# Attention over 164 keys on one core: three products of the last 36 keys in one matmul, the mean's rows ahead of the low halves, six batches' text statistics moved into batch 0

## The reference

```python
xn = layernorm(layernorm(h)) * ln_w
Q = xn[:, None] * W_qk[None, :, None]                 # 12 heads, Q = K
attn = softmax(causal(einsum('bhse,bhte->bhst', Q, Q) / sqrt(192)))
out = einsum('bhst,bhte->bhse', attn, xn[:, None] - mean(wte, axis=0))
h = h + (out / arange(1, 165)).reshape(b, s, 12 * 192) @ W_o.T
h = h + switch_moe(layernorm(h))                      # 16 experts, capacity 64, wi 192x768, wo 768x192
```

## Time and profile before

| | |
|---|---|
| median of 3 runs | 353.12 us (350.88 to 353.52) |
| the profiled execution | 352.87 us, its span 351.0 us |
| mean granted TensorE clock | 0.984 |
| PE busy | 328.0 us, 93% of the span, 2352 matmuls |
| DVE busy | 226.3 us, 64% |
| POOL busy | 166.5 us, 47% |
| ACT busy | 125.4 us, 36% |
| DMA moved | 74.35 MB, mean 212 GB/s |

### The profile page before, as it was taken

How to read it: one execution, slowest core, us unless ns; L and a number is a source line. 1 busy time by engine, 2 the same in 40 slices (tenths; PEclk the granted TensorE clock), 3 DMA queues, 4 the chain that set the end, 5 groups by cost and what they waited for, 6 DMA issues and landing times.

```text
span 351.0 us, 6745 instructions
## 1 busy us (share of the span) xinstructions
PE 328.0 (93%) x2352; PEld 304.0 (87%) x2352; DVE 226.3 (64%) x562; ACT 125.4 (36%) x437; POOL 166.5 (47%) x180
## 2 busy tenths in 40 slices
PE   8998998999999999999998996999988999999991
PEld 3696996997998998989987985999867999999991
DVE  2788696797796887787888959457676522222220
ACT  1466427434525545354362041545620111011110
POOL 3476746657559549648555013150561243334421
PEclk9999999999999999999999988999999999999997
DMA  7899997799999999999998969400136799999950
GB/s 233 250 384 276 298 335 189 146 236 247 194 229 218 233 220 202 245 229 292 210 206 237 284 193 269 110 2 1 69 124 173 209 287 256 254 257 263 258 147 11
DMA packets 21264, 74.35 MB, mean 212 GB/s; under 512 B 3452, under 2 KB 9341, under 8 KB 20474
## 3 DMA queue, kind: packets, MB, share of 16 engines
q1 hardware_dynamic: 11482, 43.22, 40.6%
q0 software_dynamic: 6800, 27.82, 38.4%
q10 hardware_dynamic: 2960, 3.04, 3.4%
HBM read 66.18 MB, written 9.25 MB: 215 GB/s over the span
## 4 chain that ended last, share of the span: by engine, by line
PE 71%; DVE 14%; DMA 4%; ACT 4%; issue 3%; SPq 1%; POOLq 0%; POOL 0%; DVEq 0%; ACTq 0%
PE bO L1279 21%; PE bS L1279 19%; PE bE L1279 14%; PE bJ L1279 11%; ACT PB L575 3%; DMA H<-in_txtA 2%; PE bT L1366 2%; DMA AwA<-dispatched 2%; DVE nwz L751 1%; DVE oTA L842 1%; DVE negmax L820 1%; PE bT L1325 1%; PE bT L1644 1%; PE bT L1370 1%; PE bT L1372 1%
## 5 line engine op out<-in xcount | busy, mean ns | idle before, releaser
L432 POOL TENSOR_TENSOR PA<-PA,rn 128x512 f32<-128x512 f32 x24 | 26.3, 1096 | 73.0 <-DVE rn L832 73.0
L410 POOL TENSOR_TENSOR AwA<-zT,w 96x512 f32<-96x512 f32 x45 | 49.7, 1175 | 16.3 <-ACT zT L552 16.3
L570 ACT ACTIVATE PA<-bS,negmax 128x128 f32<-128x128 f32 x96 | 33.9, 367 | 50.3 <-DVE negmax L820 50.2
L1279 PE MATMUL bJ<-wo_sb,oTA 128*128 128x192 f32 x288 | 51.5, 327 | 0.0
L1279 PEld LDWEIGHTS bS<-zT,AwA 96*128 96x128 f32 x384 | 48.3, 197 | 1.2
L1279 PE MATMUL bS<-zT,AwA 96*128 96x128 f32 x384 | 48.3, 280 | 0.0
L1279 PE MATMUL bO<-PA,wx 96*128 96x112 f32 x384 | 45.4, 275 | 0.9 <-DVE PA L1217 0.9
L1279 PEld LDWEIGHTS bJ<-wo_sb,oTA 128*128 128x128 f32 x288 | 46.3, 190 | 0.0
L1279 PEld LDWEIGHTS bO<-PA,wx 96*128 96x128 f32 x384 | 44.9, 192 | 1.2 <-DVE PA L1217 1.2
L479 POOL DMA_INDIRECT out<-PA,yrow x16 | 15.0, 940 | 52.0 <-DVE PA L1264 52.0
L706 ACT ACTIVATE AwA<-bO 128x448 f32<-128x448 f32 x16 | 8.7, 543 | 72.9 <-PE bO L1279 72.9
(11 more groups left out here) (259 smaller groups left out, 696.0 us busy)
## 6 DMA issues: line engine op xcount, KB each, us to landing
wbuf<-in_wte POOLq DMA_DIRECT2D x10, 1344.0 KB, 13.4
wx<-in_wte POOLq DMA_DIRECT2D x8, 1344.0 KB, 12.7
wx<-in_wi SPq DMA_DIRECT2D x16, 576.0 KB, 8.8
wx<-in_wo SPq DMA_DIRECT2D x16, 576.0 KB, 11.0
wx<-in_wte SPq DMA_DIRECT2D x12, 672.0 KB, 9.5
dispatched<-zeros SPq DMA_DIRECT2D x7, 675.5 KB, 10.4
wbuf<-in_wte SPq DMA_DIRECT2D x2, 1344.0 KB, 7.1
wx<-in_wte SPq DMA_DIRECT2D x2, 1344.0 KB, 26.9
```

The lines of the kernel that those rows point to most:

```text
L410: nc.gpsimd.tensor_tensor(o, zT[:, k, ss].unsqueeze(1).to_broadcast(list(o.shape)), w2[:, k, hs].unsqueeze(2).to_broadcast(list(o.shape)), ...
L432: nc.gpsimd.tensor_tensor(t, t, q.unsqueeze(2).to_broadcast(list(t.shape)), ALU.mult).then_inc(p_ready, 1)
L570: last = nc.scalar.activation(PA[:, h, :], bank[:, j * SA:(j + 1) * SA], ACT.Exp, bias=negmax[:, h:h + 1], accum_out=lsum[:, h:h + 1])
L1279: return nc.tensor.matmul(o, l, r, start=start, stop=stop, skip_group_check=True)
```

## The change

It has four parts.

1. `zB`, `hB` and `vB` hold the 36 rows three times (108 rows, `SR`). The text rows are loaded three times, by three DMAs each on ACT's queue where one stood. The low half of the value goes into rows 0 to 35 of the one tile `vB`; the other two copies keep the high half. `PB` gets 108 more columns, into which POOL writes the last 36 keys' normalised probabilities three times (`last_keys`, two instructions for each batch), while `normalise` 3 and 4 take 128 columns instead of 164. Round 4 of `p_transpose` turns these 108 columns over and waits for `pb_ready` instead of `p_ready`; `t_low` 4 subtracts in rows 64 to 99 alone. One matmul over `vB` and `PTB1` then gives what three gave. Two memsets of the start go.
2. In batch 6 DVE does `row_factor(LAST, 1)` ahead of `e_copy(6, 3)`, and `value_low(LAST)` behind `mean_rows` and `mean_text` instead of ahead of them.
3. `text_stats(2, 8)` moves from ahead of `row_max(0, 0)` into iteration 0, behind `e_copy(0, 1)`; `variances(2, 8)` moves from ahead of iteration 0 to behind `e_copy(0, 2)`.
4. SP no longer waits for the text rows of batches 2 to 7 ahead of its first loads of the table.

```diff
+            def last_keys():
+
+                for q0 in (0, 2):
+                    t, k = PB[:, q0:q0 + 2, SEQ:SEQ + SR].rearrange("p q (t s) -> p q t s", t=3), PB[:, q0:q0 + 2, SA:SEQ]
+                    nc.gpsimd.tensor_tensor(t, k.unsqueeze(2).to_broadcast(list(t.shape)),
+                                            rn[0:HB * SB, 12 + q0:14 + q0].unsqueeze(2).unsqueeze(3).to_broadcast(list(t.shape)),
+                                            ALU.mult).then_inc(pb_ready, 1)
...
-                        mm(oo, vA[x][:, 0:E0], PTB0[y][:, :, :], i == 0, False)
-                        last = mm(oo, vB[x][:, 0:E0], PTB1[y][:, :, :], False, i == 2)
+                        last = mm(oo, vA[x][:, 0:E0], PTB0[y][:, :, :], i == 0, False)
+                if g == 3:
+                    last = mm(oo, vB[:, 0:E0], PTB1[:, :, :], False, True)
...
-                            last = mm(ee, vB[x][:, part], PTB1[y][:, odd:HEADS:2, :], False, final)
+                    if g == 3:
+                        last = mm(ee, vB[:, part], PTB1[:, odd:HEADS:2, :], False, odd == 1)
...
-            act.dma_start(hB[:, 0:2, :], txtB[:, 0:2]).then_inc(hb_in, 16)
+            for t in range(3):
+                act.dma_start(hB[t * SB:(t + 1) * SB, 0:2, :], txtB[:, 0:2]).then_inc(hb_in, 16)
...
-            act.dma_start(hB[:, 2:NBATCH, :], txtB[:, 2:NBATCH]).then_inc(hb2_in, 16)
+            for t in range(3):
+                act.dma_start(hB[t * SB:(t + 1) * SB, 2:NBATCH, :], txtB[:, 2:NBATCH]).then_inc(hb2_in, 16)
...
-            sp.wait_ge(hb2_in, 16)
...
+                    dve.wait_ge(hb2_in, 48)
+                    text_stats(2, NBATCH)
                 e_copy(b, 2)
+                if is0(b):
+                    variances(2, NBATCH)
...
             row_max(LAST, 1)
+            row_factor(LAST, 1)
+            e_copy(b, 3)
             dve.wait_ge(ohz_ready, 3)
-            e_copy(b, 3)
-            row_factor(LAST, 1)
-            value_low(LAST)
             mean_rows()
             mean_text()
+            value_low(LAST)
```

More of the change, by code:

```diff
@@ L11 @@
 SB = SEQ - SA
+SR = 3 * SB
+LV, LP = slice(0, SB), slice(64, 64 + SB)
 EC = 96
@@ L100, in program @@
         VW = E0 + 3 * E1
-        vA, vB = ([sb(f"v{t}{x}", [128, VW], f32r) for x in "HL"] for t in "AB")
+        vA, vB = [sb(f"vA{x}", [128, VW], f32r) for x in "HL"], sb("vB", [128, VW], f32r)
         zT = sb("zT", [EC, 2, SEQ])
@@ L259, in pt_round @@
                 return PTB0[x][:, :, :], bank[:, 0:HEADS * SB].rearrange("p (h s) -> p h s", h=HEADS)
-            return PTB1[x][0:SB, :, :], bank[0:SB, 0:HEADS * SB].rearrange("p (h s) -> p h s", h=HEADS)
+            rows = LP if x else slice(0, SR)
+            return PTB1[rows, :, :], bank[rows, 0:HEADS * SB].rearrange("p (h s) -> p h s", h=HEADS)
         def o_round(b, g):
@@ L448, in iteration @@
                         add_wte(c)
+                last_keys()
                 weigh(b + 1, n, (0, 1), (2,))
@@ L574, in exps @@
                             q = 2 * (r - 3) + j
-                            last = nc.scalar.activation(PB[:, q, :], bank[0:HB * SB, j * SEQ:(j + 1) * SEQ], ACT.Exp,
+                            last = nc.scalar.activation(PB[:, q, 0:SEQ], bank[0:HB * SB, j * SEQ:(j + 1) * SEQ], ACT.Exp,
                                                         bias=negmax[0:HB * SB, 12 + q:13 + q],
@@ L926, in _ @@
             row_factor(0, 2)
-            variances(2, NBATCH)
             def b_rows(b):
@@ L1353, in p_transpose @@
             def p_transpose(b, q):
-                if q < 4:
+                if q == 4:
+                    pe.wait_ge(pb_ready, 2 * (b + 1))
+                else:
                     pe.wait_ge(p_ready, SPR * b + (q + 1 if q < 3 else SPR))
@@ L1399, in value @@
                     for i, (x, y) in enumerate(SPLIT):
-                        first, final = odd == 0 and i == 0, odd == 1 and i == 2
+                        first, final = odd == 0 and i == 0, g < 3 and odd == 1 and i == 2
                         if g < 3:
```

51 lines of the change are left out of this document (24 added, 27 removed).

## The result

The changed kernel takes 353.97 us (median of 22 runs, 352.4 to 361.08), the kernel before, on the same chips, 352.35 us (22 runs, 348.82 to 355.34). The ratio is 1.0064, with a 95% interval of 1.0042 to 1.0086: 0.6% slower, where 346.6 us had been predicted and 343.2 to 349.8 given as the range.

What follows compares the result with a forecast made beforehand. PE was taken to bound the loop, with DVE only 0.3 us ahead of it. Loop -3.6, start +0.3, sums +1.2 and mean's rows -4.2 gave -6.3 from 352.87: 346.6 us, range 343.2 to 349.8.

Steps and rivals of the forecast that it cites:

- The start, +0.3: From the start through iteration 0: 0.3 us lost in all, bounds -1.8 and +1.9.
- 348.2 us: Total time if the 432 KB more of text rows cost the start nearly their upper bound of 1.9 us.
- `factors`: DVE's step in iteration 0: its first instruction, 3.84 us before, is held by POOL again, taking 3 to 4 us.
- the first rival: Iteration 0: `factors` escapes POOL, 3.84 us shrink to 0.2; -1.5 instead of +0.3, 344.8 us; chance 0.2.
- Part 3: At batch 1's transposes: PE's wait of 0.87 us for `variances` goes, -0.9, given back later in iteration 0.
- The loop, -3.6: Five loop iterations: 0.72 us won in each, -3.6 in all, bounds -1.5 and -4.3.
- `last_keys`, 0.55 us each: POOL's two new instructions per batch: 1.1 us in all, bounds 0.4 and 1.2 each, costing nothing in the loop.
- The sums, +1.2: Batch 6, the table's sums on DVE: held longer by POOL's `weigh`, +1.2 us, bounds 0 and +1.9.
- The mean's rows, -4.2: Batch 6: PE's wait for the mean's rows shrinks and its clock stays up, -4.2 us, bounds -3.3 and -5.0.
- Batch 7, 0: Batch 7: group 3 is 0.86 us shorter, but PE then waits for `e_copy`; no gain.
- I would be wrong above all: Two signs: the four subtractions don't come earlier, or `H`'s first rows arrive over a microsecond later.

Runs made afterwards that it cites:

- e3: The kernel before, with only the four small late loads moved behind `emb_copy(0)` on ACT: 363.45 us.
- e1: The changed kernel, with ACT issuing the four small late loads straight behind its text rows, without waiting for `cst`: 346.56 us.
- e2: The changed kernel, with SP waiting for the four small late loads before it issues the table loads: 351.20 us.
- e13: The changed kernel, with the second and third copies of the text rows of batches 0 and 1 issued behind `cst`: 351.29 us.
- e6: e5 with the text rows of batches 2 to 7 issued behind the four small late loads: 349.17 us.
- e5: The changed kernel, with ACT issuing the four small late loads once the first small weights and positions have arrived: 346.06 us.
- e8: e1 without the stacked products (part 1), text rows loaded once: 348.03 us.
- e4: The kernel before, with the four small late loads issued early as in e1: 351.75 us.
- e7: e1 with the old order in batch 6, `value_low` again ahead of the mean's rows (without part 2): 349.13 us.
- e11: The kernel before, with only e10's move in POOL's order of batch 0: 350.96 us.
- e10: e5 with POOL adding the table's chunk WBUF + 2 in batch 0 behind `normalise` 1 and `weigh` 3: 344.94 us.

## Why the prediction was wrong

- **The start, +0.3: wrong by 6.8 us.** The step that failed is the sentence "The issues on ACT, two more ahead of the small loads, are hidden behind the same arrival." They are not hidden. They made `cst` 2.15 us later, the four late loads hang on `cst`, and these had 12.77 - 12.16 = 0.6 us left ahead of SP's table loads. In place of +0.3 the runs show +7.1, of which ACT's wait of 8.30 us for `flc` is the cause. I looked at what batch 0's rows wait for and did not list what else is released by ACT's queue. The margin could be read from the trace of before: the last of them was issued at 12.16 and SP's at 12.77. Nor was SP's release fixed: it, too, waits for `cst`, which became its last wait. e3 shows the step alone (+11.2), e1 and e2 its absence, and e13 with e6 that `cst`'s place in the queue moved it and not the bytes behind it.
- **That batch 0's transposes came 0.35 us later is luck, and not my 0.3.** I had all waiting for `H`'s first rows. In the changed kernel nothing waited for them. `ln`, a load of 0.8 KB behind the text rows in ACT's queue, landed 1.9 us later, and DVE worked from there to `z` without a wait. It was late by 0.35 only because the waits for `projb` (0.39) and `H` (1.28) that it had before went. DVE's timeline before:

```profile
7.00 0.18 DVE L779 TENSOR_TENSOR w<-w,ln 96x24 f32<-96x24 f32 x1 [5.15 <-DMA ln<-in_lnw]
...
10.41 0.35 DVE L765 TENSOR_TENSOR H<-bT,cS 36x192 f32<-36x192 f32 x1 [1.28 <-DMA H<-in_txtA]
```

In the changed kernel:

```profile
8.94 0.18 DVE L791 TENSOR_TENSOR w<-w,ln 96x24 f32<-96x24 f32 x1 [7.09 <-DMA ln<-in_lnw]
...
10.76 0.35 DVE L777 TENSOR_TENSOR H<-bT,cS 36x192 f32<-36x192 f32 x1
```

- **The rest of the sum stands once the queue is repaired.** With the small loads ahead of the table the times are 346.56 (e1) and 346.06 (e5), where 346.6 was forecast, and e5's start ends at 55.28, where it was 55.32 before and +0.3 was forecast.
- **The skill's rule on the queues.** I had drawn 348.2 us from the Trainium skill's "DMA: Bandwidth & Descriptors", section "Issuing engines are not separate DMA queues", by which all queues interleave on the same 16 engines. The trace agrees in kind: `flc` took 2.1 us to landing ahead of the table and 21.55 behind it, though it stands on another queue. But I had applied it to the 432 KB and not to the 0.8 KB.
- **`factors`.** "Held again", and iteration 0 ends where POOL lets it: the mechanism held, as e5 shows (3.82 us from 46.42 on). In the changed kernel itself all was late, the chunk had landed, and 0.79 us were left. Two subtractions ahead of it were held too (1.12, 0.92), and POOL's chain, now without a wait for the table, still set the end. From batch 1's to batch 2's transposes it took 25.34 us against e5's 26.30, so some 1.0 of the 1.8 us that the first rival gave for an escape came. In e8 DVE was through at 45.65, ahead of POOL's chunk at 46.06, as that rival had it, and the distance was 24.78.
- **Part 3.** The 0.9 us at batch 1's transposes is there once the start is repaired: 29.66 - 14.24 = 15.42 in e4, 27.91 - 13.53 = 14.38 in e8.
- **The loop, -3.6.** Right, and for its reason: the subtractions end 0.5 us earlier, and DVE, not PE, then sets 24.09.
- **`last_keys`, 0.55 us each.** One takes 0.82 on average, but two overlap: a pair took 1.04 to 1.49 us of POOL, where 1.1 was forecast, within the bounds. It is hidden in the loop, which takes 24.09 as forecast.
- **The sums, +1.2:** measured 0.8. **The mean's rows, -4.2:** measured -4.39, with 0.62 left of PE's wait where 0.7 was forecast. I had added 1.1 for group 3 (part 1) and 3.4 for what goes out of the way (part 2). e7 and e8 show that these are not two shares that add: part 2 is worth 4.7 alone and 2.3 on top of part 1. That group 3 itself partly runs at a clock of 0.50, which I took as given, is not the change's doing: in before it did (206.37 to 210.37 at 0.55 to 0.60), in e11, with the same instructions there, it did not, and there the clock was low for longer behind the wait instead (the stretch took 17.98 us, 18.10 in before).
- **Batch 7, 0:** right. PE's wait of the earlier trace rows grew from 0.70 to 1.55 by as much as group 3 shrank.

The forecast's range allowed the start 1.9 us at most, since the bounds were those of the bytes. No rival had a load that is late for its order, and neither of the two signs under "I would be wrong above all" came.

## What to carry to other kernels

When a change adds issues to a DMA queue, list every load behind them in that queue, what its landing releases, and how far each stands ahead of the next large transfer on any queue. A small load that falls behind megabytes costs not its own time but some of theirs. And an engine that issues DMAs behind a wait should do the work that others need first; here the traces speak for it (e10) more than the medians.
